# Fused channel attention and expert layer: fewer unread products on TensorE, k ahead of the factors and the blocks' weight slots on GpSimd, a register load moved on VectorE

## The reference, cut to what matters

```python
def xattn(q, k, v):                       # twice, with global and local vectors
    att = channel_attention(q * wq + bq, k * wk + bk, v * wv + bv, 256 ** -0.5)
    # 4 heads of 64 channels; scores are 64 x 64, summed over the 128 tokens
    return 2.0 * (att_global + att_local) * wp + bp

x = x + xattn(layernorm(x), ctx, ctx)
xf = layernorm(x)
logits = xf @ gate_w                      # top 2 of 8 experts, softmax of the two
h = gelu(xf @ w1[e] + b1[e])              # exact gelu
y = h @ w2[e] + b2[e]                     # only the two chosen experts count
x = x + sum over the two of weight * y
```

## Time and profile before

| | |
|---|---|
| median of 3 executions | 341.05 us (340.5 to 342.69) |
| profiled execution, time | 339.34 us |
| profiled execution, span | 337.5 us |
| busy share of the span | TensorE 91%, VectorE 76%, ScalarE 70%, GpSimd 51% |
| stages | attention until about 80 us, routing until about 97 us, blocks until the end |

### The profile page before, as it was taken

How to read it: one execution, slowest core, us unless ns; L and a number is a source line. 1 busy time by engine, 2 the same in 40 slices (tenths; PEclk the granted TensorE clock), 3 DMA queues, 4 the chain that set the end, 5 groups by cost and what they waited for, 6 DMA issues and landing times.

```text
span 337.5 us, 11901 instructions
## 1 busy us (share of the span) xinstructions
PE 308.4 (91%) x4073; PEld 285.6 (85%) x4073; DVE 255.8 (76%) x577; ACT 234.6 (70%) x537; POOL 173.1 (51%) x189
## 2 busy tenths in 40 slices
PE   7688898999779998999999999999999999999960
PEld 4678787998778897999999999999899999998950
DVE  8899998977879887787878778878778766656620
ACT  2599898982635887878778878778788665656530
POOL 6988989974142353544444444444444445443311
PEclk9999999999999999999999999999999999999996
DMA  7999999999610297788887977897878897888321
GB/s 250 292 337 349 320 380 372 322 395 361 240 35 18 53 294 205 231 221 261 210 264 202 277 204 236 236 272 200 249 227 234 241 249 225 234 242 235 86 31 16
DMA packets 49219, 78.56 MB, mean 233 GB/s; under 512 B 12117, under 2 KB 25625, under 8 KB 47114
## 3 DMA queue, kind: packets, MB, share of 16 engines
q1 hardware_dynamic: 39208, 66.72, 55.9%
q0 software_dynamic: 7600, 10.48, 20.1%
q10 hardware_dynamic: 2354, 0.59, 0.7%
HBM read 31.07 MB, written 9.64 MB: 121 GB/s over the span
## 4 chain that ended last, share of the span: by engine, by line
PE 68%; DMA 7%; issue 3%; DVE 3%; POOL 2%; SPq 1%; POOLq 1%; ACT 0%; DVEq 0%; ACTq 0%
PE bank L1212 29%; PE bank L1227 28%; DMA W<-in_w 3%; DMA shared<-xn_rows,row_of 3%; PE bank L1186 3%; PE bank L1086 1%; PE bank L1229 1%; DMA out<-shared,row_of 1%; PE bank L1045 1%; PE bank L1039 1%; PE bank L1061 1%; DVE W L958 1%; PE bank L1173 1%; PE bank L1104 1%; SPq L353 1%
## 5 line engine op out<-in xcount | busy, mean ns | idle before, releaser
L1227 PE MATMUL bank<-W,shared 128*128 (+1 forms) x936 | 108.5, 273 | 0.0
L1212 PE MATMUL bank<-shared,XR 128*128 128x128 f16 x1680 | 100.0, 218 | 1.9 <-issue 1.7
L1212 PEld LDWEIGHTS bank<-shared,XR 128*128 128x128 f16 x1680 | 96.7, 97 | 3.4 <-issue 2.9
L1227 PEld LDWEIGHTS bank<-W,shared 128*128 128x128 f16 x936 | 89.8, 98 | 9.9
L504 POOL DMA_INDIRECT out<-shared,row_of x39 | 61.8, 1584 | 51.2 <-ACT shared L656 24.8
L497 POOL DMA_INDIRECT shared<-xn_rows,row_of x39 | 40.6, 1042 | 89.9 <-DVE w_of L1020 72.9
L647 ACT ACTIVATE shared<-shared 128x512 f32<-128x512 f32 x78 | 49.1, 630 | 47.6 <-DVE shared L1004 37.4
L1024 DVE SCALAR_TENSOR_TENSOR shared<-shared,XP 128x512 f16<-128x512 f32 x70 | 52.4, 749 | 25.9 <-ACT shared L649 15.8
L1004 DVE SCALAR_TENSOR_TENSOR shared<-bank,XP 128x512 f32<-128x512 f32 x70 | 52.5, 750 | 20.9 <-PE bank L1212 12.3
L649 ACT ACTIVATE shared<-shared,XP 128x512 f16<-128x512 f32 x70 | 50.6, 723 | 2.3
L958 DVE SCALAR_TENSOR_TENSOR W<-W,wscale (+1 forms) x32 | 40.9, 1281 | 1.9 <-issue 1.2
(11 more groups left out here) (171 smaller groups left out, 388.8 us busy)
## 6 DMA issues: line engine op xcount, KB each, us to landing
XR<-W SPq DMA_DIRECT2D x140, 256.0 KB
W<-in_w SPq DMA_DIRECT2D x16, 1024.0 KB, 8.4
shared<-in_ctx_t SPq DMA_DIRECT2D x16, 256.0 KB, 5.7
W<-in_ctx SPq DMA_DIRECT2D x16, 128.0 KB, 7.4
out<-XR SPq DMA_DIRECT2D x16, 128.0 KB, 7.1
xn_rows<-W SPq DMA_DIRECT2D x16, 128.0 KB, 7.1
XR<-in_x SPq DMA_DIRECT2D x3, 512.0 KB, 6.1
shared<-xn_rows,row_of POOLq DMA_INDIRECT x39
```

The source lines that it names most:

```text
L1212: mm = pe.matmul(pHT[n][m][:, f % 4, :], first[:, c, w, f * P:(f + 1) * P], XT[:, n, v, c, :], start=(c == 0 and w == 0 and v == 0), stop= ...
L1227: pe.matmul(pY[n], hT[:, n, v, f, :], whole(Wh[:, slot, at:at + D]), start=(f == 0 and w == 0 and v == 0), stop=False)
```

## The change

Five edits. Ahead of the first scores 8 + 16 unread products stand in place of 26 + 16. On GpSimd the multiplication of the first k stands ahead of `factors(0, 1)`. Between the last squares and the table there are no unread products; behind the squares of experts 4, 5 and 6 there are 14 in place of 10. The register load of the first expert on VectorE stands ahead of the wait for the table. And the four small instructions and `slots_of_blocks` go from VectorE to GpSimd, as 20 instructions behind the gather of block 2, with sums in place of the reductions; in their place on VectorE come `low` 2, and `low` 3 where 2 was.

```diff
--- before.py
+++ after.py
@@ -261,6 +261,7 @@
         route = sem("route")
         gap_ok, gate_exp, mask_ok, rank_ok = sem("gap_ok"), sem("gate_exp"), sem("mask_ok"), sem("rank_ok")
         v_ok, ohr_ok, table_mm, tok_ok = sem("v_ok"), sem("ohr_ok"), sem("table_mm"), sem("tok_ok")
+        slot_step, ends_ok = sem("slot_step"), sem("ends_ok")
         perm_ok, wslot_ok, comb_ok, comb_out = sem("perm_ok"), sem("wslot_ok"), sem("comb_ok"), sem("comb_out")
         comb_step, den_ok = sem("comb_step"), sem("den_ok")
         high_ok, low_ok, param_ok, b2_ok = sem("high_ok"), sem("low_ok"), sem("param_ok"), sem("b2_ok")
@@ -420,12 +421,12 @@
                 for t in (0, 1) if i == FIRST else (t,) if 1 < t < T else ():
                     pool.wait_ge(c_in[t % NV], 16 * (t // NV + 1))
                     if t == 0:
-                        factors(0, 1)
                         pool.wait_ge(kw_in, 16)
                     after(pool, s_ok, t - 1)
                     c = CX[:, t % NV, :].rearrange("p (o d) -> p o d", o=1).broadcast_to([P, 2, D])
                     pool.tensor_tensor(k[:, t % 2], c, KW, ALU.mult).then_inc(kmul, 1)
                     if t == 0:
+                        factors(0, 1)
                         pool.wait_ge(kb_in, 16)
                     pool.wait_ge(kmul, t + 1)
                     pool.tensor_tensor(k[:, t % 2], k[:, t % 2], KB, ALU.add).then_inc(k_ok, 1)
@@ -489,8 +490,43 @@
             for n in range(NV):
                 pool.wait_ge(xn_out[n], 16 * (T // NV))
             pool.wait_ge(x1_out, 16 * T)
+            def slots_of_blocks():
+
+                planes = crossed.rearrange("p b j -> p (b j)").rearrange("p (j b) -> p j b", j=E - 1)
+                pool.wait_ge(perm_ok, 1)
+                pool.tensor_tensor(step_e[:, 0:E - 1], permf[:, 1:E], permf[:, 0:E - 1], ALU.subtract).then_inc(slot_step, 1)
+                pool.tensor_tensor(ends[:, :], key[:, :], iotaE[:, :], ALU.add).then_inc(slot_step, 1)
+                pool.wait_ge(slot_step, 2)
+                pool.tensor_tensor(ends[:, :], offs[:, :], ends[:, :], ALU.add).then_inc(ends_ok, 1)
+                pool.wait_ge(ends_ok, 1)
+                pool.tensor_tensor(eqm, eqr, ends.rearrange("p (o e) -> p o e", o=1).broadcast_to([P, E, E]), ALU.mult)\
+                    .then_inc(slot_step, 1)
+
+                for n, w in ((3, 4), (4, 2)):
+                    pool.wait_ge(slot_step, n)
+                    pool.tensor_tensor(eqm[:, :, 0:w], eqm[:, :, 0:w], eqm[:, :, w:2 * w], ALU.add).then_inc(slot_step, 1)
+                pool.wait_ge(slot_step, 5)
+                pool.tensor_tensor(endr[:, :], eqm[:, :, 0], eqm[:, :, 1], ALU.add).then_inc(slot_step, 1)
+                pool.wait_ge(slot_step, 6)
+                for j in range(E - 1):
+                    pool.tensor_scalar(planes[:, j, :], iotaB128[:, :], endr[:, j:j + 1], None, ALU.is_ge).then_inc(slot_step, 1)
+                pool.wait_ge(slot_step, 13)
+                pool.tensor_tensor(planes, planes, step_e[:, 0:E - 1].rearrange("p (j o) -> p j o", o=1)
+                                   .broadcast_to([P, E - 1, NB]), ALU.mult).then_inc(slot_step, 1)
+                pool.wait_ge(slot_step, 14)
+                pool.tensor_tensor(planes[:, 0:3, :], planes[:, 0:3, :], planes[:, 3:6, :], ALU.add).then_inc(slot_step, 1)
+                pool.wait_ge(slot_step, 15)
+                pool.tensor_tensor(planes[:, 0, :], planes[:, 0, :], planes[:, 1, :], ALU.add).then_inc(slot_step, 1)
+                pool.tensor_tensor(planes[:, 2, :], planes[:, 2, :], planes[:, 6, :], ALU.add).then_inc(slot_step, 1)
+                pool.wait_ge(slot_step, 17)
+                pool.tensor_tensor(slot_of[:, :], planes[:, 0, :], planes[:, 2, :], ALU.add).then_inc(slot_step, 1)
+                pool.wait_ge(slot_step, 18)
+                pool.tensor_scalar(wslot[:, :], slot_of[:, :], float(SPARE), None, ALU.add).then_inc(wslot_ok, 1)
+
             for i in range(-2, NB + 2):
                 b = i + 2
+                if i == 1:
+                    slots_of_blocks()
                 if b < NB:
                     after(pool, gt_ok, b - 2)
                     after(pool, got_w, b - 2)
@@ -944,11 +980,7 @@
                                   .broadcast_to([P, P, GROUP]), ALU.is_equal).then_inc(ohr_ok, 1)
 
 
-            chain(dve.tensor_tensor(ends[:, :], offs[:, :], cnt_blk[:, :], ALU.add))
-            beside(dve.tensor_tensor(step_e[:, 0:E - 1], permf[:, 1:E], permf[:, 0:E - 1], ALU.subtract))
-            chain(dve.tensor_tensor(eqm, eqr, row(ends[:, :]), ALU.mult))
-            chain(dve.tensor_reduce(endr[:, :], eqm, AX.X, ALU.add))
-
+            held = {"src": bass.ds(dve.value_load(perm[0:1, 1:2], min_val=0, max_val=E - 1), 1)}
             dve.wait_ge(table_mm, N2)
             chain(dve.tensor_scalar(tv[:, :], pTok, 0.0, slotno[:, 0:1], ALU.is_ge, ALU.mult))
             dve.scalar_tensor_tensor(out=row_of[:, :], in0=pTok, scalar=float(TOKENS), in1=tv[:, :],
@@ -959,22 +991,10 @@
                                          in1=whole(piece(dst, n, 0)), op0=ALU.mult, op1=ALU.subtract).then_inc(low_ok, 1)
 
             scales_of_second()
-            held = {"src": bass.ds(dve.value_load(perm[0:1, 1:2], min_val=0, max_val=E - 1), 1)}
             spare_slot = slice(SPARE, SPARE + 1)
             for n in range(2):
                 dve.wait_ge(high_ok, n + 1)
                 low(n, held["src"], spare_slot, wscale[:, 0, held["src"]])
-
-            def slots_of_blocks():
-
-                def by_rank(a):
-                    return a.rearrange("p (o j) -> p o j", o=1).broadcast_to([P, NB, E - 1])
-
-                chain(dve.tensor_tensor(crossed, iotaB128[:, :].rearrange("p (b o) -> p b o", o=1).broadcast_to([P, NB, E - 1]),
-                                        by_rank(endr[:, 0:E - 1]), ALU.is_ge))
-                chain(dve.tensor_tensor(crossed, crossed, by_rank(step_e[:, 0:E - 1]), ALU.mult))
-                chain(dve.tensor_reduce(slot_of[:, :], crossed, AX.X, ALU.add))
-                dve.tensor_scalar(wslot[:, :], slot_of[:, :], float(SPARE), None, ALU.add).then_inc(wslot_ok, 1)
 
             for i in range(-1, NB + 1):
                 b = i + 1
@@ -984,7 +1004,8 @@
                     dve.scalar_tensor_tensor(out=XT[:, b % 2, 1], in0=pGT, scalar=XSCALE, in1=XT[:, b % 2, 0],
                                              op0=ALU.mult, op1=ALU.subtract).then_inc(gts_ok, 1)
                 if i == -1:
-                    slots_of_blocks()
+                    dve.wait_ge(high_ok, 3)
+                    low(2, held["src"], spare_slot, wscale[:, 1, held["src"]])
                 b = i
                 converting = 1 <= i < CONVERTED - 3
                 u, g = (i - 1) % 4, (i - 1) // 4
@@ -1011,8 +1032,8 @@
                             dve.tensor_tensor(picks[:, n, :], XG[:, b % 3, D:D + E], par[:, PICK:PICK + E], ALU.mult)\
                                .then_inc(pick_ok, 1)
                         if m == 0 and i == 0:
-                            dve.wait_ge(high_ok, 3)
-                            low(2, held["src"], spare_slot, wscale[:, 1, held["src"]])
+                            dve.wait_ge(high_ok, 4)
+                            low(3, held["src"], spare_slot, wscale[:, 1, held["src"]])
                         if m == 0 and converting:
                             dve.wait_ge(high_ok, i + 4)
                             low(u, held["src"], held["dst"], wscale[:, u // 2, held["src"]])
@@ -1024,9 +1045,6 @@
                         dve.scalar_tensor_tensor(out=hT[:, n, 1, part, :], in0=hf[:, part, :],
                                                  scalar=par[:, HSC:HSC + 1], in1=hT[:, n, 0, part, :],
                                                  op0=ALU.mult, op1=ALU.subtract).then_inc(lo_ok, 1)
-                        if m == 0 and i == 0:
-                            dve.wait_ge(high_ok, 4)
-                            low(3, held["src"], spare_slot, wscale[:, 1, held["src"]])
 
         @block.tensor
         def _(pe):
@@ -1111,7 +1129,7 @@
                   .then_inc(spread, 1)
             pe.wait_ge(made, 1)
             pe.wait_ge(filled, 8)
-            keep_busy(pAT[:, 0, :], 26)
+            keep_busy(pAT[:, 0, :], 8)
             for i in range(FIRST, T - 2):
                 scores(i + 1)
                 if i < 0:
@@ -1164,8 +1182,8 @@
             pe.matmul(pCount, ones[:, :], by_expert, start=True, stop=True).then_inc(rank_ok, 1)
             for e in range(4, E):
                 squares_of_second(e)
-                keep_busy(pIdle, 10)
-            keep_busy(pIdle, 12)
+                if e < E - 1:
+                    keep_busy(pIdle, 14)
             pe.wait_ge(v_ok, 1)
             for t in range(2 * T):
                 if t % GROUP == 0:
```

## The result

| | before | changed |
|---|---|---|
| median | 341.13 us (21 executions) | 344.58 us (21 executions) |
| ratio to before | | 1.0098, 95% interval 1.0076 to 1.0119 |
| mean granted clock | 0.986 | 0.974 |

The change makes the kernel 1.0% slower; 339.3 us was forecast, with a range up to 341.2. The clocks are medians; that of the kernel before is taken from its executions beside the experiments. Without them the changed kernel's median is 343.98 us.

A forecast was written before the change was run, and what follows sets the result against it. TensorE alone bounds the kernel from 130 us on, so only that train's start can move: block 5 1.7 us earlier takes 339.34 to 337.6, and the median's 1.7 above the profiled execution gives 339.3; range for 8 in 10, 338.0 to 341.2.

The forecast's parts named there:

- D: Length of GpSimd's list of 20 instructions between two gathers: 6.5 us taken, bounds 5.3 to 10.2.
- part 4: Slots moved to GpSimd: bias of block 1 on VectorE 1.74 us earlier, block 5's weights landing near 128.4.
- the mean of 1.27 us in attention: GpSimd's average for one operation shape while VectorE is nearly always busy; taken as evidence that the list stays at 6.5.
- Formula 121.6 + D: Start of block 5's products in us when the gather of block 3 is the bound.
- The first: Rival: GpSimd's list becomes the bound at D = 7.5 to 8.5, gain 1.0 to 0, 340.0 to 341; chance 0.17.
- the second: Rival: the list from D = 8.5; at 10.2 block 5 starts 1.7 us later, 342.7; chance 0.07.
- The third: Rival: fewer unread products leave TensorE's clock low, attention ends some 2.5 us later, 341.9; chance 0.06.
- signs of being wrong: List over 8.5 us, start scores at half rate beyond 10.3 us, or w2's last landing moved over 0.5 us.
- the fourth: Rival: attention's head start carries through, last weights up to 0.9 us earlier, gain 2.6, 338.4; chance 0.18.
- by nothing or little: How far w2's last landing at 91.2 us, set by bytes, was expected to move when attention ends earlier.
- The fifth: Rival: the table waits for its one-hot tiles anyway, taking 0.3 of the 0.97 us; no chance of its own.
- Parts 1 to 3: Start: 0 counted, up to 0.9; no products ahead of table: `tv` 0.97 us earlier; register load: block 0 1.36 earlier.

The follow-up runs named there:

- e8: The kernel before with GpSimd's list done once more at the very end, beside an idle VectorE; run for its profile alone, the list took 7.1 us.
- e13: The changed kernel run again for a second profile; 343.9 us, ratio 1.0082.
- e14: The changed kernel with `low` 2 and 3 of the first expert replaced by a fill with zeros; 339.1 us, ratio 0.9989.
- e6: The changed kernel with 80 unread products in TensorE's idle time ahead of the transposes of block 3; 342.0 us, ratio 1.0027.
- e1: The changed kernel with the slots back on VectorE and both `low` in their old places; 338.7 us, ratio 0.9945.
- e5: The changed kernel with GpSimd's list moved ahead of its wait for the table; 343.2 us, ratio 1.0069.
- e10: The changed kernel with seven comparisons made one subtraction and one comparison, and the list split around the table's wait and the gathers; 338.8 us, ratio 0.9942.
- e7: The kernel before with only the first k moved ahead of the first factors on GpSimd; 340.6 us, ratio 0.9992.
- e15: The changed kernel with the list shortened and split, and the old start (42 unread products, factors ahead of first k); 338.8 us, ratio 0.9976.
- e2: The kernel before with only the list on GpSimd and the two `low` moved up; 345.9 us, ratio 1.013.
- e9: The changed kernel with one subtraction and one comparison on 273 elements for the seven comparisons, list in its place; 341.3 us, ratio 1.0031.
- e4: The kernel before with only 24 in place of 42 unread products ahead of the first scores; 339.8 us, ratio 0.9963.

## Why the prediction was wrong

**What failed** is the term D in part 4: 6.5 us for the list, 6.8 the most that costs nothing. The summing up of the instructions was nearly right, e8 measured 7.1 against 6.5. What was wrong is how much VectorE lengthens it: 11.2 us in its place. The prediction had the contention and priced it by the first multiplication by KW, a ratio of 1.16 and D = 7.5. Contention here is no ratio of GpSimd's duration. It is the other engine's time: an instruction of 0.2 us takes 1.2 when a `low` of 1.28 stands beside it. And the mean of 1.27 us in attention, which was to speak against it, was no evidence, since the long instructions that VectorE runs there (lines 755 and 764) have an input in PSUM. The timeline of the kernel before, around that first multiplication and around the gather of block 3, had the signs:

```profile
6.28 0.41 DVE L703 TENSOR_TENSOR W<-W 9x256 bf16<-9x256 f32 x1
...
6.62 0.73 DVE L755 SCALAR_TENSOR_TENSOR shared<-XR,mv,bank 128x512 f32<-128x512 f32 x1
...
107.06 1.28 DVE L958 SCALAR_TENSOR_TENSOR W<-W,wscale 128x1024 f16<-128x1024 f16 x1
107.24 1.92 POOL L497 DMA_INDIRECT shared<-xn_rows,row_of  x1 [6.15 <-DVE w_of L1020]
```

The multiplication of 1.47 us (from 6.36) had one short instruction with two inputs in SBUF beside its first 0.33 us, which fits 0.20 more. And the issue of a gather, 0.995 us in the median of all 39, took 1.92 beside a `low`. An estimate from the code and these rows would have been: two `low` within a list of 6.5 us, so D near 9.1, and with that a third `low` beside it, 10.3. Measured, the three `low` account for 3.3 of the 4.0 us. The Trainium skill ("GPSIMD Engine Reference", 8. Key points) names instructions with two SBUF inputs as one of the two kinds that contend, and the trace agrees, with 1.17 against 0.22 us for the same instruction with and without `low` beside it (e13, e14).

**The second step** that was missing is the clock. The prediction asked whether it would fall at the start, not whether it would fall behind a stall that the change itself makes. It does, and costs 1.8 us by e13's chain and 1.9 by e6. Formula 121.6 + D gives 132.8 for block 5 at D = 11.2. Measured were 133.8: the low clock adds 1.8, and the gather landed in 2.8 us in place of 3.8, most of it because its issue, with no `low` beside it now, took 1.07 us in place of 1.92.

**The rivals.** The first and the second had it that the list holds the gather of block 3, with 0.17 and 0.07; that is what happened, and neither had its size. The second's own condition, every instruction costing what 128 elements do, did not hold (7.1 us alone), and its bound from above, 10.2, was too low because it was taken from durations that had no `low` beside them. The third came in part and cost nothing that shows. In e13 the clock is up by 9.1 us and the first scores take 0.72 us. But the first scores take 1.08 to 1.12 us in e1, e5, e6 and e10, and in e5, e6 and e14 the second ones take over 1.0 in place of 0.69, where the clock is at its lower level; the transposes behind them still start at 16.1 to 16.3 us (16.49 before). So one of the signs of being wrong, scores at half rate beyond 10.3 us, came without a cost. On the fourth the profiles can't speak: e13's last squares start 0.30 us earlier (91.05 against 91.35), but that start lies anywhere between 90.96 and 93.43 us from one profile to the next, with either start, so "by nothing or little" was more than could be known. The fifth came in part: TensorE waits 0.22 us for the first tile in e13 and 0.41 in e6. From the end of the squares to `tv` it is 2.95 and 3.13 us there and 3.80 before, so the table gave 0.85 and 0.67 of its 0.97.

**What was right.** Table, register load and VectorE's chain ahead of the list, and the start in part. The timelines of e13, GpSimd's and VectorE's start, TensorE's start, and VectorE's routing:

```profile
5.34 1.27 POOL L427 TENSOR_TENSOR shared<-W,shared 128x512 f32<-128x512 f32 x1 [1.09 <-DMA shared<-in_ck]
...
5.52 1.37 DVE L735 TENSOR_TENSOR W<-W 9x256 f32<-9x256 f32 x1
```

```profile
9.14 0.72 PE L1079 MATMUL bank<-shared 128*64 128x64 f32 x16 [0.47 <-DVE shared L800]
...
13.48 0.69 PE L1079 MATMUL bank<-shared 128*64 128x64 f32 x16 [2.61 <-DVE shared L800]
```

```profile
95.08 0.26 DVE L985 TENSOR_SCALAR tv<-bank,slotno 128x39 f32<-128x39 f32 x1 [1.07 <-PE bank L1191]
...
96.89 2.48 DVE L990 SCALAR_TENSOR_TENSOR W<-W,wscale 128x1024 f16<-128x1024 f16 x2
```

The first scores come 1.3 us earlier than in the earlier trace rows and not 1.9. KW landed late, so GpSimd began at 5.34 and not 4.55; and what the scores wait for is q, not k. VectorE's L735, which has two inputs in SBUF, takes 1.37 us behind the start of GpSimd's multiplication, where it took 0.41 before (1.48 in e7, which also has k first), and q's first step starts 0.96 later, at 7.58 in place of 6.62. So the contention works the other way too. The second scores come 0.4 us earlier. `tv` is at 95.08 (95.26 said), the first `low` at 96.9 (97.2), the split of block 0 at 99.8 (100.0), `w_of` at 105.5 (105.1), the bias of block 1 at 107.85 (107.5). The 0.18 that `tv` came early is the landing's 0.30, less what the tiles took. The chain on VectorE was stepped through to within 0.4 us for 12 us; the engine that was meant to be free was not. Parts 1 to 3 together, with e1, are worth 1.6 us against the 1.7 forecast for all. That is partly luck, since the 1.7 counted on part 4 for the last step on VectorE, and e1, without part 4, was expected to win 1.0.

Of the range and chances: the measured 1.0098 lies on the edge of "within 1%", which was given 0.92, and beyond the range for 8 in 10. The cost with the widest bounds, an operation list that no row showed, was given 5.3 to 10.2 us and then a chance of 0.07 for its upper third.

## What to carry to other kernels

Before work is moved to GpSimd, list what VectorE runs in the same stretch, and count every large operation of it that reads two tensors from SBUF as time in which GpSimd may stand still: here nearly the whole of each `low`, and nothing to part of each L1045. Count the other way too: a long instruction of GpSimd that starts first holds up such an instruction of VectorE (0.41 us became 1.37, a tile of 0.68 became 1.13). Look also at what is queued behind the moved work on its new engine; here it was a gather that TensorE needs, and the stall that it made was paid twice, once as idle time and once in the clock behind it. A step that goes to an idle gap goes there only from the moment its inputs exist (e5: 7 us of gap, not 9.8), and VectorE's work beside the gap lengthens it as well. Splitting it around the transfers that the engine has to issue (e10) undid the harm here, though it won nothing over leaving the work where it was.

## What the runs showed that was not expected

- GpSimd stopped for nearly the length of a `low` on VectorE (1.28 us): 0.19 to 0.22 us became 1.17, and 2.54 became 3.77 (e8, e13). With the operation replaced by a fill, 0.22 and 2.56 (e14). The reverse is seen in e13, e7, e10 and e15.
- TensorE's clock fell within idle times of 4.9 us (e13), 5.9 us (e2) and 2.6 us (e10) and not within one of 2.4 us (e14), nor with unread products in it (e6).
- In e5, e6, e9, e10 and e14 the clock was at its lower level for 3.4 to 6.8 us from about 13 us on, around the second scores; the transposes behind them are no later for it in e5, e6 and e14. Only kernels with the new start show it, and not in every profile.
- The last weights of w2 landed up to 2.5 us apart from one profile to the next (squares from 90.96 us in e6 to 93.43 in e2), with all that follows them.
- That the 24 products alone (e4) are 0.4% faster by the ratio, 0.15% by the medians, is measured and not explained.
